# Where the weight conversions and the attention additions stand in an attention and mixture-of-experts kernel

## The reference, cut to what matters

```
scores = einsum('ti,ei->te', xt, gate_w); probs = softmax(scores)
expert_weights, expert_indices = top_k(probs, 2); expert_weights /= sum
x1 = silu(einsum('ti,eoi->teo', xt, w1)); x3 = einsum('ti,eoi->teo', xt, w3)
expert_outs_all = einsum('teo,eio->tei', x1 * x3, w2)
```

## Time and profile before

| What | us |
|---|---|
| median of 3 runs | 303.94 (302.26 to 304.8) |
| the profiled execution's own time | 301.63 |
| its span | 299.9 |
| PE busy | 242.4 (81%) |
| DVE busy | 189.9 (63%) |
| ACT busy | 152.0 (51%) |
| POOL busy | 135.3 (45%) |

### The profile page before, as it was taken

One profiled execution on the slowest core, in us unless ns is written; L12 is line 12 of the kernel. 1 busy time (PEld: TensorE's weight loads), 2 busy tenths in 40 slices (PEclk: granted clock), 3 DMA queues, 4 the chain that ended last, 5 costly groups with the idle time before them and its releaser, 6 DMA issues.

```text
span 299.9 us, 6061 instructions
## 1 busy us (share of the span) xinstructions
PE 242.4 (81%) x1784; PEld 158.6 (53%) x1784; DVE 189.9 (63%) x413; ACT 152.0 (51%) x255; POOL 135.3 (45%) x128
## 2 busy tenths in 40 slices
PE   0327998996678886999999999999999979989400
PEld 0117776874455443576666666666566545555200
DVE  3998799499874798685859586867674323333000
ACT  2876784186568661736374545455564323434100
POOL 6375000173300005667874672747265564316561
PEclk9999799999977997999999999999999999999765
DMA  6999992088935339999999999899989999797552
GB/s 209 412 420 407 424 427 107 0 212 237 183 59 76 59 78 119 139 177 146 170 170 130 153 210 127 119 138 178 181 107 152 147 172 124 132 150 109 82 58 32
DMA packets 86290, 50.48 MB, mean 168 GB/s; under 512 B 72547, under 2 KB 83811, under 8 KB 85061
## 3 DMA queue, kind: packets, MB, share of 16 engines
q1 hardware_dynamic: 76516, 35.42, 52.7%
q0 software_dynamic: 9744, 14.69, 32.1%
HBM read 23.35 MB, written 11.67 MB: 117 GB/s over the span
## 4 chain that ended last, share of the span: by engine, by line
PE 29%; DMA 13%; DVE 9%; issue 8%; POOLq 6%; ACT 5%; POOL 1%; ACTq 0%; DVEq 0%
PE bank L1144 16%; PE bank L1157 8%; DMA out<-regions,row_out 5%; POOLq L452 5%; DMA out<-xn 4%; DVE regions L748 3%; ACT regions L527 3%; PE bank L1196 3%; DMA xrow<-xrow 2%; DMA out<-area,row_out 2%; DVE xrow L940 2%; PE bank L1173 1%; PE bank L1185 1%; POOL out L461 1%; DVE xrow L945 1%
## 5 line engine op out<-in xcount | busy, mean ns | idle before, releaser
L1144 PE MATMUL bank<-regions,xg_all 128*128 x468 | 108.9, 384 | 3.9 <-DMA xg_all<-regions 2.1
L1144 PEld LDWEIGHTS bank<-regions,xg_all 128*128 128x128 f16 x468 | 44.6, 99 | 54.7 <-issue 8.2
L1157 PE MATMUL bank<-regions,xrow 128*128 x468 | 59.7, 280 | 7.5 <-DMA xrow<-xrow 7.4
L1157 PEld LDWEIGHTS bank<-regions,xrow 128*128 128x128 f16 x468 | 46.1, 100 | 21.7 <-issue 10.6
L613 ACT ACTIVATE xrow<-xrow 128x512 f16<-128x512 f32 x39 | 24.6, 630 | 58.5 <-DVE xrow L940 58.5
L940 DVE SCALAR_TENSOR_TENSOR xrow<-bank,xrow 128x512 f32<-128x512 f32 x39 | 26.9, 691 | 38.4 <-PE bank L1144 35.2
L461 POOL DMA_INDIRECT out<-area,row_out x20 | 33.6, 1680 | 30.9 <-issue 13.3
L461 POOL DMA_INDIRECT out<-regions,row_out x19 | 31.2, 1643 | 28.7 <-issue 17.5
L439 POOL DMA_INDIRECT xrow<-xsplit,row_in x8 | 11.3, 1408 | 66.4 <-DMA xg_all<-xrow 33.4
L945 DVE TENSOR_TENSOR xrow<-xrow 128x512 f16<-128x512 f32 x39 | 26.9, 690 | 21.6 <-ACT xrow L613 21.6
L608 ACT ACTIVATE xrow<-bank 128x512 f32<-128x512 f32 x39 | 23.2, 595 | 27.7 <-PE bank L1144 27.5
(11 more groups left out here) (150 smaller groups left out, 304.1 us busy)
## 6 DMA issues: line engine op xcount, KB each, us to landing
regions<-wexp SPq DMA_DIRECT2D x8, 1536.0 KB, 13.9
xsplit<-xrow SPq DMA_DIRECT2D x4, 512.0 KB, 9.6
out<-xn POOLq DMA_DIRECT2D x8, 256.0 KB
area<-x SPq DMA_DIRECT2D x2, 768.0 KB, 7.7
regions<-wattn SPq DMA_DIRECT2D x1, 1032.0 KB, 10.6
xrow<-xrow SPq DMA_TRANSPOSE x39
area<-x SPq DMA_DIRECT2D x1, 512.0 KB, 3.5
regions<-xsplit,row_in POOLq DMA_INDIRECT x31, 4.7
```

The source lines that it names most:

```text
L1144: last = mm(bank_[:], xg[t % 4][:, KD * d + k, :], w16[:, bass.ds(e, 1), w, at:at + I].rearrange("p a c -> p (a c)"), start=(k == 0 and n ...
L1157: last = mm(ps_y[t % 2][:, 0:D], hT[t % 2][:, IC * d + c, :], w16[:, bass.ds(e, 1), w, at:at + D].rearrange("p a c -> p (a c)"), start=(c ...
```

## The change

EARLY becomes 6: `hi(5)` and `expert_lo(5)` go to the front, on ACT behind `halves(7)` and ahead of the Silu table load and `kv_halves(1)`, on DVE behind `kv_lo(1)`. Experts 6 and 7 are converted in halves of 1536 words, one half in each of steps 0 to 3. `hi_half(t)` stands behind `h_hi(t)` on ACT, where `hi` had stood ahead of `silu(t)`; `expert_lo_half(t)` stands at the end of DVE's step, where `expert_lo` had stood. They count on semaphores of their own. And the groups of attention additions stand two adds earlier, PAIR_AT + 2 in place of + 4. A short description that came with the change names adds 12, 18, 24 and 27; PAIR_AT is not touched, and the expression in the diff gives 9, 15, 21 and 27. This document goes by the diff.

```
-EARLY = 5
+EARLY = 6
+HALF = WCOLS // 2
 PAIR_AT = [4 + 3 * p for p in range(NP)]
-FIN_AFTER = {PAIR_AT[2 * i + 1] + 4: (2 * i, 2 * i + 2) for i in range(NP // 2)}
+FIN_AFTER = {PAIR_AT[2 * i + 1] + 2: (2 * i, 2 * i + 2) for i in range(NP // 2)}
@@ POOL, gather
                 if t == 2 * FEW:
-                    pool.wait_ge(w_lo, E)
+                    pool.wait_ge(late_lo, 2 * (E - EARLY))
@@ ACT
+            def hi_half(n):
+                e, part = EARLY + n // 2, slice(HALF * (n % 2), HALF * (n % 2 + 1))
+                act.wait_ge(raw_loaded[e], 16)
+                act.wait_ge(w_lo, e - 1)
+                a.activation(w16[:, e, 0, part], raw(e)[:, part], ACT.Copy, scale=SCALE).then_inc(late_hi, 1)
@@ ACT, end of the front
             halves(7)
+            act.wait_ge(w_lo, 4)
+            hi(5)
             a.activation(warm[:], log_scale[:], ACT.Silu).then_inc(warm_done, 1)
             kv_halves(1)
@@ ACT, y_out
                 if t == 4:
-                    act.wait_ge(w_lo, 7)
+                    act.wait_ge(late_lo, 2)
@@ ACT, tile steps
             for t in range(ST + 2):
-                if t < E - EARLY:
-                    act.wait_ge(w_lo, EARLY - 1 + t)
-                    hi(EARLY + t)
...
                 if t < ST:
                     h_hi(t)
+                if t < 2 * (E - EARLY):
+                    hi_half(t)
@@ DVE
+            def expert_lo_half(n):
+                e, part = EARLY + n // 2, slice(HALF * (n % 2), HALF * (n % 2 + 1))
+                dve.wait_ge(late_hi, n + 1)
+                v.scalar_tensor_tensor(w16[:, e, 1, part], regions[:, (e + 2) * WCOLS:(e + 3) * WCOLS][:, part], SCALE,
+                                       w16[:, e, 0, part], ALU.mult, ALU.subtract).then_inc(late_lo, 1)
...
             kv_lo(1)
+            expert_lo(5)
@@ DVE, tile steps
-                if t < E - EARLY:
-                    expert_lo(EARLY + t)
+                if t < 2 * (E - EARLY):
+                    expert_lo_half(t)
@@ PE, hidden
-                if t < E:
+                if t < EARLY:
                     pe.wait_ge(w_lo, t + 1)
+                elif t < E:
+                    pe.wait_ge(late_lo, 2 * (t + 1 - EARLY))
```

More of the change, by code:

```diff
@@ L216, in build @@
         w_lo = sem("w_lo")
+        late_hi = sem("late_hi")
+        late_lo = sem("late_lo")
         shift_ready = sem("shift_ready")
```

## The result

The changed kernel takes 308.83 us (median of 20 runs, 304.3 to 313.08) against 304.23 us for the kernel before in the same comparison (20 runs): +4.6 us, ratio 1.0156, 95% interval 1.0109 to 1.0203.

The account below looks back on a forecast made before the run. The prediction took POOL's queue from add 2 on to bound the kernel. Front +2.2 and groups +2.1 sum to +4.3 us, from the median 303.94 to 308.2 us, 1.4% slower; its own range 304 to 311, widened to 301.5 to 311.

Parts of the forecast that it names:

- POOL's chain: From add 2 to the end, POOL's queue of adds, gathers and waits for landings sets the time.
- The front, +2.2 us: Conversions before step 4 on DVE: 2.13 from expert 5 plus 0.07 from steps 0 to 3, delaying add 2.
- statistics: Attention pair 0's statistics, step 4 on DVE, start 2.2 us later than before.
- The groups, +2.1 us: Attention groups at adds 9, 15, 21 and 27 on POOL: 6.27 + 2.58 - 6.78, from which wait is shared.
- The new separate wait: At add 23 on POOL, no longer shared with a group: costs an interval of 6.27 us.
- The wait at 9: On POOL, now shared by group and expert 2's first add: saves 6.78 us, less 2.58 for two gathers.
- the drain in front of the group: On POOL, at each of four groups: the same before and after the change, so it drops out.
- The eight result buffers are no limit.: Evictions on ACT: tile t needs add t-8, and add 15 lands before tile 23's eviction at 220.40.
- the signs on POOL's timeline: Add 2 near 126.4, add 11 near its old time, long intervals at 13, 18, 23, 28, 32, add 38 near 296.5.
- The cheap wait: Rival, chance 0.28: add 23's wait is cheap or DVE's delay not fully passed on; 306.6 or 305.5 us.
- Faster: Rival, chance 0.14: adds 9 to 27 land sooner, meeting fewer transposes; 295 us, or 300 for two thirds of it.
- The short description's positions: Rival, chance 0.03: groups at adds 12, 18, 24 and 27, only the front term left, 306.1 us.

Follow-up runs that it names:

- the two single-number edits: Kernel before with the third group in front of add 24, not 23: 307.24 us; or the second in front of 18, not 17: 300.89; before 304.05.
- its two comparisons: Kernel before with only the conversions changed, groups left at 11, 17, 23 and 29: 304.80 us against 304.05, again 306.95 against 302.06.
- the groups alone: Kernel before with only the groups moved, to adds 9, 15, 21 and 27, conversions as before: 305.7 us over 18 runs, before 303.8.

## Why the prediction was right

**What bounds the kernel.** POOL's chain, not PE: shown by the two single-number edits, by the lag of 8 to 15 us at add 38 wherever the groups are present, and by its fall to 2.5 us without them. The chain of waits had pointed at PE for the middle of the run. One sentence of the prediction is wrong: POOL does not only fall behind from add 8 on. Its distance to the evictions was 23 us at add 29, and from add 32 (20.1 us) it shrank to the 8.5 of the end, because adds 32 to 38 follow each other by some 2.1 us and the evictions by 4.0. The end stayed POOL's all the same.

**The front, +2.2 us.** Right, step by step: `h_mul(0)` +2.1 (2.1), steps 4.43 us (4.46), statistics +2.0 (2.2), add 2 +2.1 (2.2), all less the 0.6 us of the execution's later front. In the four traces with these conversions add 2 is 1.5 to 2.4 us later. In time this part is less sure: +0.8 and +4.9 in its two comparisons. The reason given, that DVE comes too late to its idle time because ACT's table load and `kv_halves` stand behind `hi(5)`, is shown by the kernel that puts `expert_lo(5)` first.

**The groups, +2.1 us.** The sum came out (+1.9 over all runs of the groups alone), but in part by luck: both terms came out dearer than priced, and shorter waits elsewhere, for which there was no term, made up for it. The new separate wait was priced at an interval of 6.27 us; it took 6.21 in the changed kernel's trace and 6.7 in the mean of the six. The wait at 9 was to save 6.78 - 2.58 = 4.20, which is 2.05 more than a plain interval; by the stretch from add 8 to add 12 it saved 0.2 at most. The step that failed is the drain in front of the group and what follows it: I took the drain as equal on both sides, but behind add 8 it took 5.9 in the mean and 5.1 in front of a group at 11, and adds 9 to 12 then followed 2.7 us apart (2.6 in the changed kernel) and not 2.1. Against that, the stretches from add 12 to 18 and from 24 to 38 became 1.0 and 1.2 us shorter, six traces against three; the prediction had no term for that. The five stretches from add 2 to add 38 (cut at 8, 12, 18 and 24) sum to 0.2 - 0.2 - 1.0 + 4.1 - 1.2 = +1.9 us.

**The wait at the first add.** The separate ones at 13, 18, 23, 28 and 32 took 4.3 to 7.8 us over all traces with groups. By the Trainium skill, DMA: Bandwidth & Descriptors, "Anatomy of one DMA — SWDGE (gpsimd) path", the landing of 128 KB would be estimated at 2.3 us. The traces do not agree: even at the end of the changed kernel, add 31 to add 32 is 4.65 us, of which 1.55 is the issue and 3.10 the wait behind it, and PE had finished 2.4 us before that wait ended. The measured wait decides.

**"The eight result buffers are no limit."** Wrong as a statement, without effect on the sum: tiles 35 to 37 wait up to 2.52 us for a buffer. Had POOL not been later still, this would have been the next wait.

**Not foreseen.** The interval from add 3 to add 4 is 7.3 us in the mean of the seven traces with halved conversions (5.9 to 7.7) and 6.2 in the seven without (5.7 to 7.3). It makes about 0.8 us from add 2 to add 8, and its cause was not tried. Two of the signs on POOL's timeline missed with it: add 11 was to come near its old time and came 5.1 us later (182.63 and not 177.57, with 0.6 of it the later front), and add 38 was to come near 296.5 and came at 299.57. In this pair of executions the chain from add 2 on grew by 4.8 us, where the prediction had 2.1; the medians, over 20 runs each, are what agree with it.

**The rivals.** The cheap wait did not hold: 6.2 us at add 23. Faster held in small part: the separate waits at 13, 18, 28 and 32 were each 0.4 to 0.9 us shorter with the groups of the change (means of six traces against three), 2.1 us together, where this rival needed 7.4. The short description's positions were not what ran: the groups stand in front of 9, 15, 21 and 27.

## What to carry to other kernels

When one queue issues DMAs with waits between them, number its entries and read it as a chain of its own: a queue at 45% busy can set the end. Two waits for the same landing cost one if they stand at the same entry, so it is not earlier or later that counts for a group, but which entry it meets. A wait that other work already fills is worth nothing when shared: the one at add 9, with two gathers inside it, gave back 0.2 us at most, where those at 18 and 23 gave 2.5 to 4. Before a piece of work is moved into idle time, look at what ends that idle time; if it is an engine to which half of the same work was just added, the idle time is no longer where it was.

## What the runs showed of the hardware

- An add by indirect DMA with accumulation, 128 rows of 1 KB, holds POOL's queue for 1.8 to 2.3 us from one add to the next where little or nothing is awaited (adds 32 to 38, in all 13 traces with groups), of which 1.55 are the instruction.
- Without the eight accumulating DMAs of 256 KB and their waits the evictions of tiles 8 to 38 took 130.2 us, against 131.9 to 138.1 in the 13 traces with them, and the difference lies in the last 15 tiles. It is one trace. Whether DMA traffic or the wait for result buffers was behind it is open.
- The end of the front (`kv_blocks(1)`) came between 92.4 and 97.8 us in 14 traces, so some 5 us of the spread of single runs can arise before the first tile step.
